# A fused test-time-memory and expert kernel: its router by VectorE's top-8 sort and first-match marking, and gates by tanh, in place of exponentials and chained reductions

## The chip, the cores and the metric

The kernel runs on one core of one Trainium2 chip. The metric is the device time of one execution in microseconds (us), and every time here is of that kind or a position in one profiled execution. A core has five engines with queues of their own: TensorE (PE; its weight loads are PEld), VectorE (DVE), ScalarE (ACT), GpSimd (POOL) and SyncE (SP), which issues the DMAs. They meet only at semaphores.

## The reference

2,048 tokens with 128 features pass through two layers, each as `x = x + layernorm(f(layernorm(x)))`. The first `f` is a memory that takes one training step on the tokens (forward, gradients, AdamW) and is then read with the new weights. The second is a mixture of 8 experts, of which each token uses 2. What concerns this case is how those two are chosen and weighted:

```python
z = _layernorm(x, ln_g, ln_b)
logits = jnp.einsum('bth,he->bte', z, rW) + rb
probs = jax.nn.softmax(logits, axis=-1)
topv, topi = jax.lax.top_k(probs, TOP_K)              # TOP_K = 2, E = 8
mask = jnp.sum(jax.nn.one_hot(topi, E) * topv[..., None], axis=-2)
w = mask / jnp.maximum(jnp.sum(mask, axis=-1, keepdims=True), 1e-08)
hid = jax.nn.gelu(jnp.einsum('bth,ehf->btef', z, W1) + b1, approximate=False)
outs = jnp.einsum('btef,efh->bteh', hid, W2) + b2
return x + jnp.sum(outs * w[..., None], axis=2)
```

The kernel computes all eight experts for every token and adds them with the weights `w`, six of which are zero.

## The kernel before, in words

The tokens form four blocks (`NB = 4`) of 512, each of four tiles (`TB = 4`) of 128 tokens. Every engine has one program, written out by hand in order, and waits on semaphores; nothing is reordered by a planner. Operations of VectorE that depend on each other are joined by a semaphore of its own (`step`, `link`, lines 709 to 719).

There are three stages. First the memory's forward and backward passes over the four blocks. Then a hinge: AdamW's new weights and, for block 0, everything that the experts need. Then 32 expert slots (`STEPS = NB * E`), which start two early (`AHEAD = 2`): in slot s TensorE makes the hidden layer of expert step s+2 (`hidden`, two halves of three 512-column products each), then the output of step s (`output`, 16 products of 128 columns), ScalarE applies Gelu to each half (`gelu`, line 682), and VectorE adds the output with its weight (`add_expert`, line 1009, four instructions at L1020). `hidden` of a block waits for `z_lo`, the low part of its normalised tokens (`z_low`, line 913, recorded at L915).

The router of a block has these steps. TensorE makes the logits in bank 4 (`logits`, line 477, recorded as L330 with `late_sb`). VectorE adds the bias and subtracts the greatest logit (`shift_logits`, line 927: L931, L935, L936). ScalarE takes exponentials of 32 values per partition (`exponentials`, line 662). VectorE then makes the weights (`route`, line 939, L960 to L994): a chain of maxima, comparisons and a rank by a descending ramp, which marks the first of equal values, with the sums and reciprocals beside it (L953). Last, TensorE transposes the weights (`w_transpose`, line 484, recorded as L487), ScalarE copies them out (`wT_out`) and TensorE multiplies them with the biases (`b2_term`).

For block 0 these steps stand in the hinge. VectorE's order there is written at lines 1051 to 1064: `... retrieve2(1); retrieve2(2); shift_logits(0); z_low(0); route(0); retrieve2(3)`. For the blocks 1 to 3 they are spread over the expert slots of the block before: `due(position, slot)` tells in which slot of that block a step is placed. Logits are at 3, `shift_logits` at 4, exponentials at 5, the first seven pieces of `route` at 5, the rest at 6, and `w_transpose` at 7. In each slot VectorE runs `add_expert` first, then what is due. In slot 6 `norm_r` of the block after the next one stands before the rest of `route` (for blocks 1 and 2; there is none for block 3).

Of the kernel before, what the change touches and what calls it, by code (L numbers as in the profile page):

```python
# [15 lines left out]
ALU = mybir.AluOpType  # L16
# [27 lines left out]
def memory_and_experts(nc, x, early, late, fW1, fW2, out):  # L44
# [19 lines left out]
    with ExitStack() as ctx:  # L64
# [58 lines left out]
        def part(pack, at, name):  # L123
# [20 lines left out]
        ramp = sb("ramp", [P, TB, E])  # L144
        lg, ex, pr, eq, oh1, oh2 = (kT[:, i * T * E:(i + 1) * T * E].rearrange("p (t e) -> p t e", e=E)
                                    for i in range(6))
        w_tok = sb("w_tok", [P, T, E])
        red = kT[:, 6 * T * E:7 * T * E].rearrange("p (i t) -> p i t", t=T)
# [6 lines left out]
        zeroed, ident_ready, half_ready, table_ready, ramp_ready = (sem(n) for n in (  # L155
            "zeroed", "ident_ready", "half_ready", "table_ready", "ramp_ready"))
# [21 lines left out]
        lg_mm, lg_shift, ex_ready, w_ready, w_tr, wT_ready = (sem(n) for n in (  # L178
            "lg_mm", "lg_shift", "ex_ready", "w_ready", "w_tr", "wT_ready"))
# [48 lines left out]
        NORM_R, RESIDUAL, NORM_Z, Y_STATS, Y_NORM, Z_LOW, LOGITS_SHIFT, ROUTE = -2, -1, 0, 1, 2, 2, 4, (5, 6)  # L228
        R_TR, Z_TR, LOGITS, EXP, W_TR, B2_TERM = -2, 2, 3, 5, 7, 8
# [55 lines left out]
        def _(pool):  # L285
# [7 lines left out]
            def rsqrt(ln, b, where=None):  # L293
# [11 lines left out]
            pool.iota(ramp[:], pattern=[[0, TB], [-1, E]], base=E, channel_multiplier=0,  # L305
                      allow_small_or_imprecise_dtypes=True).then_inc(ramp_ready, 1)
# [267 lines left out]
        def _(act):  # L574
# [87 lines left out]
            def exponentials(b):  # L662
                act.wait_ge(lg_shift, b + 1)
                act.activation(tok(ex, b), tok(lg, b), ACT.Exp).then_inc(ex_ready, 1)
# [14 lines left out]
            exponentials(0)  # L679
# [9 lines left out]
            for slot in range(-AHEAD, STEPS):  # L689
                if slot + AHEAD < STEPS:  # L690
                    for c in range(C):
                        gelu(C * (slot + AHEAD) + c)
                if slot == 0:
                    wT_out(0)
                if due(Z_TR, slot):
                    zT_out(due(Z_TR, slot))
                if due(EXP, slot):
                    exponentials(due(EXP, slot))
                if due(W_TR, slot):
                    wT_out(due(W_TR, slot))  # L700
# [3 lines left out]
        def _(dve):  # L704
# [21 lines left out]

            def advance(pieces, count):
                for _ in range(count):
                    next(pieces, None)
# [189 lines left out]
            def wide(v):  # L919
                return v.unsqueeze(2).to_broadcast([P, TB, E])  # L920

            def small(i, b):
                return red[:, i, span(b)]

            MX, SM, RS, M1, F1, M2, F2, DN = range(8)

            def shift_logits(b):
                if b == 0:
                    dve.wait_ge(ramp_ready, 1)
                dve.wait_ge(lg_mm, b + 1)  # L930
                dve.tensor_tensor(tok(lg, b), bank[4][:, 0:TB * E].rearrange("p (t e) -> p t e", e=E),  # L931
# [3 lines left out]
                yield from link(dve.tensor_reduce(small(MX, b), tok(lg, b), AX_X, ALU.max))  # L935
                dve.tensor_tensor(tok(lg, b), tok(lg, b), wide(small(MX, b)),  # L936
                                  ALU.subtract).then_inc(lg_shift, 1)

            def route(b):


                e, p, q, first, second = (tok(v, b) for v in (ex, pr, eq, oh1, oh2))
                total, inverse, top, rank, top2, denom = (small(v, b) for v in (SM, RS, M1, F1, M2, DN))
                done = {}

                def chain(ins):
                    done["chain"] = step(ins)

                def side(make, *operands, **kw):

                    if "side" in done:
                        dve.wait_ge(dve_step, done["side"])
                    done["side"] = step(make(*operands, **kw))  # L953

                def chained():
                    yield
                    dve.wait_ge(dve_step, done["chain"])

                dve.wait_ge(ex_ready, b + 1)
                chain(dve.tensor_reduce(top, e, AX_X, ALU.max))  # L960
                side(dve.tensor_reduce, total, e, AX_X, ALU.add)
                yield from chained()
                chain(dve.tensor_tensor(q, e, wide(top), ALU.is_equal))
                side(dve.reciprocal, inverse, total)
                yield from chained()
                chain(dve.tensor_tensor(q, q, ramp[:], ALU.mult))
                side(dve.tensor_tensor, p, e, wide(inverse), ALU.mult)
                yield from chained()
                chain(dve.tensor_reduce(rank, q, AX_X, ALU.max))
                yield from chained()  # L970
                chain(dve.tensor_tensor(first, q, wide(rank), ALU.is_equal))
                yield from chained()
                chain(dve.scalar_tensor_tensor(out=e, in0=first, scalar=-2.0, in1=e, op0=ALU.mult,
                                               op1=ALU.add))
                yield from chained()
                chain(dve.tensor_reduce(top2, e, AX_X, ALU.max))
                yield from chained()
                chain(dve.tensor_tensor(q, e, wide(top2), ALU.is_equal))
                side(dve.tensor_tensor, denom, top, top2, ALU.add)
                yield from chained()  # L980
                chain(dve.tensor_tensor(q, q, ramp[:], ALU.mult))
                side(dve.tensor_tensor, denom, denom, inverse, ALU.mult)
                yield from chained()
                chain(dve.tensor_reduce(rank, q, AX_X, ALU.max))
                side(dve.tensor_scalar, denom, denom, 1e-8, None, ALU.max)
                yield from chained()
                chain(dve.tensor_tensor(second, q, wide(rank), ALU.is_equal))
                side(dve.reciprocal, denom, denom)
                yield from chained()
                chain(dve.tensor_tensor(first, first, second, ALU.add))  # L990
                side(dve.tensor_tensor, p, p, wide(denom), ALU.mult)
                yield
                dve.wait_ge(dve_step, done["side"])
                dve.tensor_tensor(tok(w_tok, b), p, first, ALU.mult).then_inc(w_ready, 1)  # L994

# [65 lines left out]
            run(shift_logits(0))  # L1061
# [3 lines left out]
            for slot in range(-AHEAD, STEPS):  # L1065
# [16 lines left out]
                if due(LOGITS_SHIFT, slot):  # L1082
                    run(shift_logits(due(LOGITS_SHIFT, slot)))
                if due(ROUTE[0], slot):
                    routing = route(due(ROUTE[0], slot))
                    advance(routing, 7)
                if due(ROUTE[1], slot):
                    run(routing)
# [42 lines left out]
```

## Time and profile before

| | |
|---|---|
| median of 3 runs | 206.26 us (206.22, 206.26, 208.02) |
| the profiled execution | 204.86 us |
| its span, first to last instruction | 203.1 us |
| busy: PE / PEld | 178.0 / 140.8 us |
| busy: DVE / ACT / POOL | 145.4 / 99.1 / 22.1 us |
| mean granted TensorE clock | 0.99 |

The span leaves out what lies before the first and behind the last instruction: 1.8 us in this execution. Busy time is not the limit by itself: an engine's idle time counts only where the chain of work that ended last passes through it. "L330" is line 330 of the kernel; where a helper issues the instruction, all its uses carry the helper's line, and the names of the tiles tell them apart.

### The profile page before, as it was taken

The page shows a single profiled execution, that of the slowest core. Times are in us where ns is not written, and L with a number is a line of the kernel's source. Part 1 is how long each engine was busy: PE and PEld are TensorE (multiplying, and loading weights), DVE is VectorE, ACT ScalarE, POOL GpSimd, SP SyncE. Part 2 cuts the span into 40 slices and gives each one's busy share as a digit, 9 for nine tenths or more (in the row PEclk, how much of TensorE's full clock was granted, in tenths as well). Part 3 has the DMA queues.
Part 4 walks back from the last instruction along what each step waited for, and adds up shares of the span by engine and source line. Part 5 has one row for each costly group of instructions (what it writes and reads, how often), then busy time and mean ns, then how long its engine had stood idle before and what let it go on. Part 6 is the DMA issues. An engine that isn't in the chain of part 4 may idle for free.

```text
span 203.1 us, 3196 instructions
## 1 busy us (share of the span) xinstructions
PE 178.0 (88%) x1089; PEld 140.8 (69%) x1089; DVE 145.4 (72%) x564; ACT 99.1 (49%) x150; POOL 22.1 (11%) x30
## 2 busy tenths in 40 slices
PE   7388988897988796999999999999999999999930
PEld 7334454465644484879999699988799897889920
DVE  0987695879685799979348977668976656475474
ACT  2157682946444309934567326384355495334200
POOL 1440000000000140032000131001211000010010
PEclk9999999999999999999999999999999999999996
DMA  5970000000000000000000000100000100001001
GB/s 153 342 233 4 0 0 3 0 0 0 0 3 2 0 2 0 3 0 0 3 0 2 0 3 0 52 3 0 2 0 3 52 0 3 2 2 52 3 0 52
DMA packets 3232, 4.96 MB, mean 24 GB/s; under 512 B 240, under 2 KB 1552, under 8 KB 3216
## 3 DMA queue, kind: packets, MB, share of 16 engines
q1 hardware_dynamic: 3216, 4.76, 7.2%
q8 instruction: 9, 0.15, 0.3%
q14 instruction: 7, 0.06, 0.1%
HBM read 3.71 MB, written 1.05 MB: 23 GB/s over the span
## 4 chain that ended last, share of the span: by engine, by line
PE 69%; DVE 17%; ACT 7%; issue 3%; DMA 2%; POOL 0%; POOLq 0%; DVEq 0%; ACTq 0%
PE bank L330 65%; DVE stats L737 3%; PE bank L338 2%; DMA x_tok<-in_x_dram 2%; ACT sig L580 2%; DVE xnT L1020 2%; ACT nsig L587 2%; DVE mv L740 1%; DVE s L870 1%; DVE s L878 1%; DVE xnT L874 1%; DVE vT L881 1%; ACT s L580 1%; ACT alrT L580 1%; ACT kT L576 1%
## 5 line engine op out<-in xcount | busy, mean ns | idle before, releaser
L1020 DVE SCALAR_TENSOR_TENSOR xnT<-bank,w_tok,xnT 128x128 f32<-128x128 f32 x128 | 36.0, 344 | 27.7 <-PE bank L330 27.3
L297 POOL TENSOR_TENSOR rstd<-vpe,minus_half 128x4 f32<-128x4 f32 (+1 forms) x21 | 20.7, 995 | 175.5 <-DVE vpe L745 162.0
L330 PE MATMUL bank<-z_hi,fW_hi 128*128 128x512 f32 x64 | 27.8, 435 | 1.5 <-DVE z_lo L915 1.5
L330 PE MATMUL bank<-z_lo,fW_hi 128*128 128x512 f32 x64 | 25.2, 394 | 0.0
L330 PE MATMUL bank<-z_hi,fW_lo 128*128 128x512 f32 x64 | 25.0, 390 | 0.0
L330 PEld LDWEIGHTS bank<-fW_sb,sig 128*128 128x128 f32 x192 | 22.8, 192 | 2.2 <-ACT h1T L686 1.5
L330 PE MATMUL bank<-fW_sb,sig 128*128 128x128 f32 x192 | 23.4, 276 | 0.0
L686 ACT ACTIVATE sig<-bank,early_sb 128x512 f32<-128x512 f32 x24 | 16.2, 688 | 13.8 <-PE bank L330 13.7
L686 ACT ACTIVATE k_tok<-bank,early_sb 128x512 f32<-128x512 f32 x20 | 13.5, 688 | 15.4 <-PE bank L330 15.3
L330 PEld LDWEIGHTS bank<-fW_sb,k_tok 128*128 128x128 f32 x160 | 19.3, 191 | 1.5 <-ACT sig L686 0.8
L330 PEld LDWEIGHTS bank<-fW_sb,h1T 128*128 128x128 f32 x160 | 19.3, 191 | 1.5 <-ACT k_tok L686 0.8
L330 PE MATMUL bank<-fW_sb,h1T 128*128 128x128 f32 x160 | 19.6, 275 | 0.0
L330 PE MATMUL bank<-fW_sb,k_tok 128*128 128x128 f32 x160 | 19.6, 275 | 0.0
L686 ACT ACTIVATE h1T<-bank,early_sb 128x512 f32<-128x512 f32 x20 | 13.5, 688 | 12.3 <-PE bank L330 12.2
L330 PE MATMUL bank<-xnT,early_sb 128*128 128x512 f32 x24 | 11.9, 606 | 2.9 <-ACT alrT L580 1.3
L330 PEld LDWEIGHTS bank<-z_hi,fW_hi 128*128 128x128 f32 x64 | 12.1, 190 | 3.0 <-issue 1.6
L409 PEld LDWEIGHTS bank<-ident 128*128 128x128 f32 x93 | 11.8, 155 | 3.1 <-issue 1.6
L330 PEld LDWEIGHTS bank<-z_lo,fW_hi 128*128 128x128 f32 x64 | 12.0, 188 | 2.9
L409 PE MATMUL bank<-ident 128*128 128x128 f32 x93 | 12.5, 296 | 1.5 <-POOL ident L288 1.5
L330 PEld LDWEIGHTS bank<-z_hi,fW_lo 128*128 128x128 f32 x64 | 12.2, 190 | 1.5
L580 ACT ACTIVATE s<-bank,bn 128x512 f32<-128x512 f32 x8 | 5.5, 687 | 11.0 <-PE bank L330 11.0
L330 PEld LDWEIGHTS bank<-xnT,early_sb 128*128 128x128 f32 x24 | 4.0, 190 | 7.3 <-issue 5.7
(129 smaller groups left out, 270.4 us busy)
## 6 DMA issues: line engine op xcount, KB each, us to landing
x_tok<-in_x_dram SPq DMA_DIRECT2D x4, 256.0 KB, 4.4
fW_raw<-in_fW_dram SPq DMA_DIRECT2D x1, 1024.0 KB, 9.2
out_dram<-xn_tok SPq DMA_DIRECT2D x3, 256.0 KB, 2.5
early_sb<-in_early_dram SPq DMA_DIRECT2D x1, 268.0 KB, 4.1
late_sb<-in_late_dram SPq DMA_DIRECT2D x1, 264.0 KB, 4.8
out_dram<-xn_tok SPq DMA_DIRECT2D x2, 128.0 KB, 2.0
b_diag<-in_late_dram SPq DMA_DIRECT2D x4, 4.0 KB
fW_sb<-in_fW_dram SPq DMA_DIRECT2D x1, 0.5 KB, 11.7
```

The lines of the kernel that those rows point to most:

```text
L297: pool.tensor_tensor(rstd[:, ln, where], vpe[:, ln, where], minus_half[:, 0:where.stop - where.start], ALU.pow).then_inc(rstd_ready[ln], 1)
L330: return pe.matmul(out_, lhsT, rhs, start=start, stop=stop)
L338: last = pe.transpose(bank[7][:, i * P:(i + 1) * P], pieces(i), ident[:])
L409: pe.transpose(bank[scratch][:, 0:P], ident[:], ident[:])
L576: act.activation(dst, src, ACT.Identity, **kw).then_inc(s, 1)
L580: act.activation(cut(into, b), source[:], ACT.Sigmoid, bias=bias).then_inc(s, 1)
L587: act.activation(into[:, slot * BLOCK:(slot + 1) * BLOCK], cut(sig, b), ACT.Identity, scale=-1.0, bias=1.0).then_inc(s, 1)
L686: act.activation(g_buf[n % G_RING], bank[H_BANK[n % len(H_BANK)]][:], ACT.Gelu, bias=col(FB1 + n % UB)).then_inc(g_done, 1)
L737: last = dve.bn_stats(stats[:, t, :], source(i, t))
L740: last = dve.bn_aggr(mv[:, ln, t, :], stats[:, t, :])
L870: dve.scalar_tensor_tensor(out=cut(r_sig1, b), in0=bank[RZ1[b]][:], scalar=bn[:, 0:1], in1=cut(r_sig1, b), op0=ALU.add, op1=ALU.mult).then ...
L1020: last = dve.scalar_tensor_tensor(out=y_tok[:, t, :], in0=bank[Y_BANK[m % len(Y_BANK)]][:, i * P:(i + 1) * P], scalar=w_tok[:, t, e:e + 1] ...
```

## The change

The router's method is replaced. VectorE adds the bias, sorts the eight logits of each tile with one `max` per tile (eight values out, in falling order), copies the first two into a row whose other six places hold -3.0e38, and runs one `match_replace` per tile, which puts +3.0e38 in place of the first match of each of the eight values in the row of logits. That row is 14 wide, with six places of -3.0e38 for the fillers to match. What is now greater than the logit was chosen. The weight of a chosen expert is 0.5 * (1 + tanh(logit - half the sum of the two chosen logits)), which is its share of the two. So ScalarE takes a tanh (`Tanh`, in place, 32 values per partition) instead of exponentials, and `route` is one instruction. The tiles are arrays of their own and no longer lie in `kT`; GpSimd fills two of them once (`memset`) where it made the ramp before (`iota`).

The places: `choose(0)` stands where `shift_logits(0)` stood, ahead of `z_low(0)`; `route(0)` stays behind it. For the other blocks `choose` is at 4, the tanh at 5 and the one-instruction `route` at 5, in place of slots 5 and 6. `w_transpose` stays at 7.

```diff
-        ramp = sb("ramp", [P, TB, E])
-        lg, ex, pr, eq, oh1, oh2 = (kT[:, i * T * E:(i + 1) * T * E].rearrange("p (t e) -> p t e", e=E)
-                                    for i in range(6))
+        TOP_K, SORTED = 2, 8
+        NO_MATCH = -3.0e38
+        lg = sb("lg", [P, T, E + SORTED - TOP_K])
+        ranked = sb("ranked", [P, T, SORTED])
+        chosen = sb("chosen", [P, T, SORTED])
+        marked = sb("marked", [P, T, E + SORTED - TOP_K])
+        gate = sb("gate", [P, T, E])
+        picked = sb("picked", [P, T, E])
+        pair_sum = sb("pair_sum", [P, T])
...
-        NORM_R, RESIDUAL, NORM_Z, Y_STATS, Y_NORM, Z_LOW, LOGITS_SHIFT, ROUTE = -2, -1, 0, 1, 2, 2, 4, (5, 6)
-        R_TR, Z_TR, LOGITS, EXP, W_TR, B2_TERM = -2, 2, 3, 5, 7, 8
+        NORM_R, RESIDUAL, NORM_Z, Y_STATS, Y_NORM, Z_LOW, CHOOSE, ROUTE = -2, -1, 0, 1, 2, 2, 4, 5
+        R_TR, Z_TR, LOGITS, GATE, W_TR, B2_TERM = -2, 2, 3, 5, 7, 8
...
-            pool.iota(ramp[:], pattern=[[0, TB], [-1, E]], base=E, channel_multiplier=0,
-                      allow_small_or_imprecise_dtypes=True).then_inc(ramp_ready, 1)
+            pool.memset(lg[:], NO_MATCH).then_inc(rest_ready, 1)
+            pool.memset(chosen[:], NO_MATCH).then_inc(rest_ready, 1)
...
-            def exponentials(b):
-                act.wait_ge(lg_shift, b + 1)
-                act.activation(tok(ex, b), tok(lg, b), ACT.Exp).then_inc(ex_ready, 1)
+            def gate_tanh(b):
+                act.wait_ge(gate_in, b + 1)
+                act.activation(tok(gate, b), tok(gate, b), ACT.Tanh).then_inc(gate_ready, 1)
...
-            def shift_logits(b):
+            def choose(b):
+
                 if b == 0:
-                    dve.wait_ge(ramp_ready, 1)
+                    dve.wait_ge(rest_ready, 2)
                 dve.wait_ge(lg_mm, b + 1)
-                dve.tensor_tensor(tok(lg, b), bank[4][:, 0:TB * E].rearrange("p (t e) -> p t e", e=E),
+                dve.tensor_tensor(lg[:, span(b), 0:E], bank[4][:, 0:TB * E].rearrange("p (t e) -> p t e", e=E),
                                   rb_b.unsqueeze(1).to_broadcast([P, TB, E]), ALU.add).then_inc(lg_read, 1)
                 yield
                 dve.wait_ge(lg_read, b + 1)
-                yield from link(dve.tensor_reduce(small(MX, b), tok(lg, b), AX_X, ALU.max))
-                dve.tensor_tensor(tok(lg, b), tok(lg, b), wide(small(MX, b)),
-                                  ALU.subtract).then_inc(lg_shift, 1)
+                for t in tiles(b):
+                    last = dve.max(ranked[:, t, :], lg[:, t, 0:E])
+                yield from link(last)
+                copied = step(dve.tensor_scalar(chosen[:, span(b), 0:TOP_K], ranked[:, span(b), 0:TOP_K], 1.0, None,
+                                                ALU.mult))
+                yield from link(dve.tensor_tensor(pair_sum[:, span(b)], ranked[:, span(b), 0],
+                                                  ranked[:, span(b), 1], ALU.add))
+                dve.scalar_tensor_tensor(out=tok(gate, b),
+                                         in0=pair_sum[:, span(b)].unsqueeze(2).to_broadcast([P, TB, E]),
+                                         scalar=-0.5, in1=lg[:, span(b), 0:E], op0=ALU.mult,
+                                         op1=ALU.add).then_inc(gate_in, 1)
+                dve.wait_ge(dve_step, copied)
+                for t in tiles(b):
+                    last = dve.match_replace(marked[:, t, :], chosen[:, t, :], lg[:, t, :], -NO_MATCH)
+                yield from link(last)
+                yield from link(dve.tensor_tensor(tok(picked, b), marked[:, span(b), 0:E], lg[:, span(b), 0:E],
+                                                  ALU.is_gt))
+                yield from link(dve.tensor_scalar(tok(picked, b), tok(picked, b), 0.5, None, ALU.mult))
 
             def route(b):
-                e, p, q, first, second = (tok(v, b) for v in (ex, pr, eq, oh1, oh2))
...
-                dve.tensor_tensor(tok(w_tok, b), p, first, ALU.mult).then_inc(w_ready, 1)
+                dve.wait_ge(gate_ready, b + 1)
+                dve.scalar_tensor_tensor(out=tok(w_tok, b), in0=tok(gate, b), scalar=1.0, in1=tok(picked, b),
+                                         op0=ALU.add, op1=ALU.mult).then_inc(w_ready, 1)
+                yield
...
-            run(shift_logits(0))
+            run(choose(0))
             z_low(0)
             run(route(0))
...
-                if due(LOGITS_SHIFT, slot):
-                    run(shift_logits(due(LOGITS_SHIFT, slot)))
-                if due(ROUTE[0], slot):
-                    routing = route(due(ROUTE[0], slot))
-                    advance(routing, 7)
-                if due(ROUTE[1], slot):
-                    run(routing)
+                if due(CHOOSE, slot):
+                    run(choose(due(CHOOSE, slot)))
+                if due(ROUTE, slot):
+                    run(route(due(ROUTE, slot)))
```

## Rows read from the trace of the kernel before

**Rows 1.** The page: span, and part 1, busy time, share, instructions by engine

```profile
span 203.1 us, 3196 instructions
PE 178.0 (88%) x1089; PEld 140.8 (69%) x1089; DVE 145.4 (72%) x564; ACT 99.1 (49%) x150; POOL 22.1 (11%) x30
```

**Rows 2.** The chain that ended last: start us, us, what; hinge, and slots 6 and 7

```profile
79.57 0.20 DVE kT L931
79.79 0.20 DVE kT L935
...
80.21 0.61 DVE z_lo L915
...
80.96 1.63 PE bank L330 x6
...
113.02 0.20 DVE w_tok L994
...
113.27 0.28 PE bank L487
```

**Rows 3.** Who waited for whom: us in total, times, longest us

```profile
PE bank L330 <- DVE z_lo L915: 1.5, 1, 1.5
...
PE bank L487 <- DVE w_tok L994: 0.7, 2, 0.4
```

**Rows 4.** Timeline, all engines, hinge: start, us, engine, line, operation [idle before, releaser]

```profile
78.51 0.95 PE L330 MATMUL bank<-late_sb,alrT 128*128 128x8 f32 x8
...
79.56 1.28 ACT L664 ACT_TABLE_LOAD   x1
79.57 0.19 DVE L931 TENSOR_TENSOR kT<-bank,late_sb 128x32 f32<-128x32 f32 x1
...
80.12 0.69 DVE L915 TENSOR_TENSOR z_lo<-alrT,z_hi 128x512 fp32r<-128x512 f32 x1
...
80.96 0.47 PE L330 MATMUL bank<-z_hi,fW_hi 128*128 128x512 f32 x1 [1.50 <-DVE z_lo L915]
81.11 1.28 ACT L686 ACT_TABLE_LOAD   x1
```

**Rows 5.** VectorE's groups, shapes apart: line, operation, shapes, count, busy us, mean ns

```profile
L740 DVE BATCH_NORM_AGGREGATE mv<-stats 128x2 f32<-128x6 f32 x64 | 6.1, 157 | 0.5
...
L971 DVE TENSOR_TENSOR kT<-kT 128x32 f32<-128x32 f32 x4 | 0.8, 192 | 0.1
```

**Rows 6.** Timeline of VectorE: four L740 in a row, then the next, dependent one

```profile
73.71 0.38 DVE L740 BATCH_NORM_AGGREGATE mv<-stats 128x2 f32<-128x6 f32 x4
74.12 0.17 DVE L905 TENSOR_SCALAR vpe<-mv 128x4 f32<-128x4 f32 x1
```

**Rows 7.** Timeline of TensorE: last output before w_transpose, blocks 1 and 3

```profile
110.98 1.95 PE L330 MATMUL bank<-fW_sb,sig 128*128 128x128 f32 x16
113.27 0.28 PE L487 MATMUL bank<-ident,w_tok 128*32 128x128 f32 x1 [0.35 <-DVE w_tok L994]
...
168.61 1.95 PE L330 MATMUL bank<-fW_sb,k_tok 128*128 128x128 f32 x16
170.39 0.27 PE L487 MATMUL bank<-ident,w_tok 128*32 128x128 f32 x1
```

**Rows 8.** Timeline, block 1's slots 4 and 5: ScalarE's load, VectorE's additions

```profile
104.05 0.18 DVE L931 TENSOR_TENSOR kT<-bank,late_sb 128x32 f32<-128x32 f32 x1
...
105.10 1.28 ACT L664 ACT_TABLE_LOAD   x1
...
106.18 1.13 DVE L1020 SCALAR_TENSOR_TENSOR xnT<-bank,w_tok,xnT 128x128 f32<-128x128 f32 x4 [1.50 <-PE bank L330]
```

**Rows 9.** Stretches at the end: stretch, length, busy of each engine, PEclk, DMA share, GB/s

```profile
196.00:198.00 2.00, 0.00 (x0) 0.00 (x0) 1.25 (x11) 0.00 (x0) 0.97 (x2) 1.00 0.00 0
198.00:200.00 2.00, 0.00 (x0) 0.00 (x0) 1.57 (x8) 0.00 (x0) 0.39 (x1) 0.79 0.00 0
200.00:203.00 3.00, 0.00 (x0) 0.00 (x0) 0.48 (x2) 0.00 (x0) 0.00 (x0) 0.50 0.26 87
```

More of the change, by code:

```diff
@@ L143, in memory_and_experts @@
         minus_half = sb("minus_half", [P, TB])
-        ramp = sb("ramp", [P, TB, E])
-        lg, ex, pr, eq, oh1, oh2 = (kT[:, i * T * E:(i + 1) * T * E].rearrange("p (t e) -> p t e", e=E)
-                                    for i in range(6))
+        TOP_K, SORTED = 2, 8
[7 more added lines that the diff above has]
+        pair_sum = sb("pair_sum", [P, T])
         w_tok = sb("w_tok", [P, T, E])
-        red = kT[:, 6 * T * E:7 * T * E].rearrange("p (i t) -> p i t", t=T)
         x_in = [sem(f"x_in{i}") for i in range(NB)]
@@ L153, in memory_and_experts @@
         out_done = sem("out_done")
-        zeroed, ident_ready, half_ready, table_ready, ramp_ready = (sem(n) for n in (
-            "zeroed", "ident_ready", "half_ready", "table_ready", "ramp_ready"))
+        zeroed, ident_ready, half_ready, table_ready, rest_ready = (sem(n) for n in (
+            "zeroed", "ident_ready", "half_ready", "table_ready", "rest_ready"))
         b2_zeroed, b2_in, fw_hi_done, fw_lo_done = (sem(n) for n in (
@@ L177, in memory_and_experts @@
                              "zT_ready", "zhi_done", "zlo_done"))
-        lg_mm, lg_shift, ex_ready, w_ready, w_tr, wT_ready = (sem(n) for n in (
-            "lg_mm", "lg_shift", "ex_ready", "w_ready", "w_tr", "wT_ready"))
+        lg_mm, gate_in, gate_ready, w_ready, w_tr, wT_ready = (sem(n) for n in (
+            "lg_mm", "gate_in", "gate_ready", "w_ready", "w_tr", "wT_ready"))
         rs1_done, rs2_done, shift_ready, lg_read, dp_done = (sem(n) for n in (
@@ L678, in _ @@
             rsig2_out(3)
-            exponentials(0)
+            gate_tanh(0)
             def gelu(n):
@@ L696, in _ @@
                     zT_out(due(Z_TR, slot))
-                if due(EXP, slot):
-                    exponentials(due(EXP, slot))
+                if due(GATE, slot):
+                    gate_tanh(due(GATE, slot))
                 if due(W_TR, slot):
@@ L725, in run @@
                     pieces = [p for p in pieces if next(p, "end") != "end"]
-            def advance(pieces, count):
-                for _ in range(count):
-                    next(pieces, None)
             def span(b):
@@ L916, in z_low @@
                                   ALU.subtract).then_inc(zlo_done, 1)
[L919 to L925, printed above, removed]
-            def shift_logits(b):
+            def choose(b):
                 if b == 0:
-                    dve.wait_ge(ramp_ready, 1)
+                    dve.wait_ge(rest_ready, 2)
                 dve.wait_ge(lg_mm, b + 1)
-                dve.tensor_tensor(tok(lg, b), bank[4][:, 0:TB * E].rearrange("p (t e) -> p t e", e=E),
+                dve.tensor_tensor(lg[:, span(b), 0:E], bank[4][:, 0:TB * E].rearrange("p (t e) -> p t e", e=E),
                                   rb_b.unsqueeze(1).to_broadcast([P, TB, E]), ALU.add).then_inc(lg_read, 1)
@@ L934, in shift_logits @@
                 dve.wait_ge(lg_read, b + 1)
-                yield from link(dve.tensor_reduce(small(MX, b), tok(lg, b), AX_X, ALU.max))
-                dve.tensor_tensor(tok(lg, b), tok(lg, b), wide(small(MX, b)),
-                                  ALU.subtract).then_inc(lg_shift, 1)
-            def route(b):
-                e, p, q, first, second = (tok(v, b) for v in (ex, pr, eq, oh1, oh2))
[L943 to L991, printed above, removed]
@@ L992, in route @@
                 yield
-                dve.wait_ge(dve_step, done["side"])
-                dve.tensor_tensor(tok(w_tok, b), p, first, ALU.mult).then_inc(w_ready, 1)
             def start_sum(j):
```

## The prediction

> **What bounds the kernel now.** I read the page first. TensorE is busy 88% of the span, VectorE 72%, ScalarE 49% [rows 1]. No share says what an edit of the router is worth; that takes the places where the chain of waits passes through the router. There are two kinds. In the hinge the chain runs through VectorE: the bias addition at 79.57, the maximum at 79.79, then `z_low` of block 0, and from 80.96 through TensorE's first hidden product [rows 2]. In the expert slots it is on TensorE, except for the end of `route`: it passes w_tok (L994) at 113.02 and reaches w_transpose at 113.27 [rows 2].
>
> The list of waits gives the size. Once TensorE waits for z_lo, 1.5 us, and twice for w_tok, 0.7 us together [rows 3]. In the expert part, from 81 to 194, TensorE has no other wait in that list. So ScalarE's and VectorE's work in there is hidden, and only these three waits can answer to the edit.
>
> The timeline of the hinge shows that the first wait is one of VectorE alone. TensorE ends its logits at 78.51 + 0.95 = 79.46 and sits still until 80.96; the table load and exponentials on ScalarE lie beside that [rows 4].
>
> **The change part by part. First, `choose(0)` ahead of `z_low(0)`.** Before, z_low starts at 80.12, which is 0.55 us after the bias addition [rows 4]: two dependent steps and the start of the third instruction. Afterwards all of `choose` comes first, as `run` goes through to its end, and the last step waits as well.
>
> The prices come from small operations. A dependent step of 32 values starts 0.22 us after the one before it (79.57 to 79.79) [rows 2]; the durations behind this are 192 ns for 32 values and 157 ns for the smallest forms [rows 5]. Without dependence they overlap: four of 157 ns take 0.38, so each starts (0.38 - 0.16) / 3 = 0.075 after the last, and the dependent one follows 0.03 after the end [rows 6]. No row shows a `max` or a `match_replace`. I take them as records of some 8 to 16 values, about 165 ns, starting 0.08 apart, nearest to the 157 ns rows. A match_replace I count as two records, since it has to take in eight values to look for before it passes the row. That gives:
>
> bias addition 0.22; four max 3 x 0.08 + 0.20 = 0.44; the copy 0.08 and the dependent pair sum 0.19, 0.27; the tanh's input 0.11; eight records of match_replace 7 x 0.08 + 0.20 = 0.76; the comparison and the halving 0.45. The sum is 2.25 us.
>
> So z_low starts 2.25 - 0.55 = 1.70 us later, and so does the first hidden product, since nothing else is due later: TensorE stands idle already. From below, a match_replace is one record like L740, and so is a max: 0.22 + 0.41 + 0.27 + 0.11 + 0.41 + 0.45 = 1.87, a delay of 1.3. From above, none of the twelve overlap and each takes a whole dependent step of 0.22: 0.22 + 0.88 + 0.27 + 0.11 + 1.76 + 0.45 = 3.69, a delay of 3.1. I take 1.70, nearer to the lower end, because all small operations in the rows overlap.
>
> On the two records there is a sentence in the Trainium skill, page VectorE: DVE Perf Modes, section "Two Vector instructions with no wait between them": it lists `MATCH_VALUE_LOAD` and `MATCH_REPLACE_8` as two instructions with one input each. No row here shows either. By one record for each match_replace at 0.08 the sum would be 1.93 and the delay 1.4; by the page it stays as above.
>
> **Second, w_transpose at slot 7.** Before, the second half of `route` ran in slot 6 behind norm_r and ended at 113.2 in block 1. From the start of the last output products to w_transpose takes 113.27 - 110.98 = 2.29 us there, and 170.39 - 168.61 = 1.78 in block 3, where no norm_r stands before it and TensorE does not wait [rows 7]. Block 2 repeats block 1 (2.30). So the two waits cost 0.51 and 0.52: their ends on the list are shorter (0.35 each), because the overlap with the product before is lost too. Afterwards w_tok of block 1 is ready in slot 5: `choose` starts at about 104.05 [rows 8] and ends near 106.3; the tanh's input is there about 1.1 us after the start, at 105.2, when ScalarE is just through with its two Gelus (it began its load at 105.10 [rows 8]); tanh ends at 105.5; and `route`, one instruction behind the additions at 106.18 to 107.31, ends by 107.7, five us ahead of w_transpose. Both stalls go: -1.03 us. Behind them the list has nothing that is late next.
>
> What `choose` pushes back in slot 4: the additions of slot 5 started at 106.18 after 1.50 us of idle waiting for TensorE [rows 8], so 2.25 us of work from 104.05 makes them some 0.15 late. The output that needs their bank begins at 110.98 [rows 7], over three us after they end, so this costs nothing; even 3.7 us of work would leave two.
>
> **Third, ScalarE.** Four loads of 1.28 us before the exponentials and four behind them, back to Gelu's table, may go wholly or down to one. In the hinge the load back ends at 81.11 + 1.28 = 82.39 [rows 4] while hidden products run from 80.96; TensorE's list shows no wait for a Gelu there. In the slots it idles anyway, and TensorE waits for none [rows 3]. I take 0. Should tanh still need loads, the load and tanh end at about 106.6 in block 1, before `route` comes up at 107.3; in the hinge the first hidden product ends after 83 and the loads before it. Also 0, so this term doesn't depend on the tables.
>
> The rest: VectorE has some 24 router records per block before and 19 after, and in the hinge route(0) shrinks from 3 us to 0.2. That follows z_low, where TensorE did not wait for it, so it only widens the margin in front of the first w_transpose. GpSimd's two fills stand where the ramp stood, far ahead of 79.5. Both 0.
>
> **Sum.** +1.70 - 1.03 = +0.67 us. The profiled execution takes 204.86, its span 203.1 and 1.8 around it; it becomes 205.5. The median of the runs is 1.4 higher at 206.26, and the forecast is made against it: 206.9 us.
>
> **The rivals.** (A) The clock falls in the hinge: the case on the other side, slower by over 1%. TensorE's idle time there grows from 1.5 to 3.2 us. At the end of the kernel the last product ends at about 194.5; the granted clock is still 1.00 until 198, 0.79 on average from 198 to 200, and 0.50 behind that [rows 9], so it fell to its lower level (1.2 of 2.4 GHz) some 4.6 us after the last work. 3.2 us is less, but these rows hold one fall only, and TensorE's work before this gap is thinner than at the end. The upper end of my delay, 3.1, would make the gap 4.6 us, just there. From that point the first slots run at half speed. The price: from 80.96 to the end of the first output at 87.40 TensorE has 6.4 us of dense work; half to all of 3.2 us of it twice over adds 1.6 to 3.2, say 2.4. With the delay that is 206.26 + 0.67 + 2.4 = 209.3; with the slow instructions as well 210.7. Chance 0.10. The page TensorE: Matmul & The Clock Gate of the Trainium skill, section "HAM oscillation — how this bites in real kernels", warns of this kind of idle gap in TensorE's work; the rows here show the gate closing only at the end.
>
> (B) Sorting and marking are dear, without a fall of the clock: a delay of 2.3 to 3.1, net +1.3 to +2.1, some 207.9. For it: a sort of eight is not like any operation in the rows. Chance 0.15.
>
> (C) They are cheap, or the hinge hides part: a delay of 1.0 to 1.3. Net 0 to +0.3, time 206.4. It speaks for it that the least shapes give 1.87 us. Chance 0.15.
>
> (D) VectorE's total counts, not the place: 5 records per block fewer, and 1.0 us from w_transpose, and the hinge pays under 0.5 because z_low is overtaken by something I have not seen. Then it is faster, by 0.5 to 1.5 us: 205.2. Against it: z_low is the only releaser of the first hidden product in the list [rows 3]. The page VectorE: DVE Perf Modes, section "Rules for kernel authors", says to minimise the count of chained operations; by count alone this change should gain. Chance 0.08, and half of that or more within 1%.
>
> (E) The stalls at w_transpose remain, because tanh is late or w_tok is held: +1.7, 208.0. The margin of five us speaks against it. Chance 0.05.
>
> The forecast itself holds 0.47, with its own range of 206.5 to 207.4.
>
> **How the numbers follow.** About 1%, 2.1 us, is what a measurement of this kernel can tell from no change. Faster by more than that needs (D) beyond its own bound or runs that scatter: 0.04. Slower by more, from 208.3: (A), the end of (B), some of (E), 0.14. Within: 0.82. The range takes (C) and most of (B) and (D), and leaves out most of (A): 205.6 to 208.6.
>
> **What would show it.** In the changed profile: z_low of block 0 starting 2.0 to 2.5 us after the bias addition and the wait for z_lo grown from 1.5 to about 3.2; no wait for w_tok in the list and 1.78 us from the last output's start to each w_transpose; no table load between Gelus, or loads without any effect; granted clock 1.00 from 80 to 90. I am wrong if a max or a match_replace lasts over 0.2 us, if the delay in the hinge is below 1.0, or if the clock falls there.

## The result and the profile after

| | before | after |
|---|---|---|
| median of 16 runs each | 205.75 us | 206.85 us |
| lowest | 204.49 us | 205.16 us |
| ratio, with its 95% interval | | 1.0077 [1.0049, 1.0106] |
| profiled execution / its span | 204.86 / 203.1 us | 207.73 / 205.9 us |
| mean granted clock of that execution | 0.99 | 0.97 |

The change makes the kernel 0.8% slower by the ratio, 1.6 us, and 1.1 us by the two medians; the forecast was 0.3% slower. Runs of one kernel lie in groups, and this case can't be read without them: of the kernel before, seven of 16 took 204.5 to 204.8 us, the others 205.7 and more; of the changed kernel one took 205.16, nine 206.6 to 206.9, and the rest more. The reason, as far as the profiles show it, is TensorE's clock, below.

The page of the changed kernel, span and part 1, answers to [rows 1]:

```profile
span 205.9 us, 3171 instructions
PE 181.2 (88%) x1089; PEld 143.4 (70%) x1089; DVE 141.1 (69%) x544; ACT 90.6 (44%) x143; POOL 22.3 (11%) x31
```

VectorE has 20 instructions and 4.3 us less to do, ScalarE 8.5 us less, and the span is longer. TensorE has the same 1,089 products and is busy 3.2 us longer with them: its products became slower, and the forecast's sum had no term for that (its rival (A) had).

The chain that ended last, in the hinge (start us, us, what), answers to [rows 2]:

```profile
80.34 0.20 DVE lg L925
80.54 0.02 issue
80.56 0.39 DVE ranked L930 x4
80.95 0.02 issue
80.97 0.17 DVE chosen L932
81.14 0.08 DVE pair_sum L934
81.22 0.02 issue
81.24 0.19 DVE gate L936
81.44 0.58 DVE marked L942 x5
82.02 0.02 issue
82.04 0.20 DVE picked L944
82.24 0.02 issue
82.27 0.19 DVE picked L946
82.46 0.02 issue
82.48 0.70 DVE z_lo L916
83.18 0.14 issue
83.32 1.91 PE bank L335 x6
85.22 0.85 PE bank L467 x4
86.08 3.67 PE bank L335 x12
89.74 0.11 PE bank L492
```

The whole of `choose` now stands in the chain in front of z_low, step by step. From the bias addition to z_low it is 82.48 - 80.34 = 2.14 us, where it was 0.55 [rows 4]: a delay of 1.59. The list of TensorE's waits from 79 us to 200 us, which answers to [rows 3], has one line left:

```profile
PE bank L335 <- DVE z_lo L916: 3.1, 1, 3.1
```

It grew from 1.5 to 3.1, and both waits for w_tok are gone. The timeline of TensorE at the end of slot 7 in block 1 answers to [rows 7]: 116.72 - 114.93 = 1.79 us, as block 3 had before, instead of 2.29. Blocks 2 and 3 of the changed kernel have 1.78.

```profile
114.93 1.95 PE L335 MATMUL bank<-fW_sb,sig 128*128 128x128 f32 x16
116.72 0.27 PE L492 MATMUL bank<-ident,w_tok 128*32 128x128 f32 x1
```

The clock is what the sum lacked. The stretches of the changed kernel around the hinge (stretch, length, busy us of PE, PEld, DVE, ACT, POOL with counts, PEclk, DMA share, GB/s):

```profile
80.00:82.00 2.00, 0.23 (x3) 0.14 (x2) 1.88 (x17) 0.82 (x3) 0.00 (x0) 1.00 0.00 0
82.00:84.00 2.00, 0.68 (x3) 0.63 (x4) 1.86 (x7) 1.00 (x1) 0.00 (x0) 1.00 0.00 0
84.00:86.00 2.00, 2.00 (x10) 1.62 (x9) 0.66 (x1) 1.37 (x2) 0.00 (x0) 0.62 0.03 8
86.00:88.00 2.00, 2.00 (x7) 1.56 (x6) 1.44 (x9) 0.60 (x1) 0.29 (x1) 0.53 0.00 0
88.00:90.00 2.00, 2.00 (x12) 1.60 (x11) 1.25 (x6) 1.68 (x4) 0.71 (x1) 1.00 0.00 0
```

From 84.5 to 87.9 the clock is at its lower level, 1.2 of 2.4 GHz (a mean of 0.62 is 1.5 us at half, one of 0.53 is 1.9 us). It falls 4.3 us after TensorE's last work at 80.23, and when it falls TensorE has been at work again for 1.2 us. The first w_transpose in the timeline of TensorE, of the kernel before:

```profile
85.62 0.27 PE L487 MATMUL bank<-ident,w_tok 128*32 128x128 f32 x1
```

and of the changed kernel:

```profile
89.58 0.27 PE L492 MATMUL bank<-ident,w_tok 128*32 128x128 f32 x1
```

From the first hidden product to it the changed kernel takes 89.58 - 83.32 = 6.26 us, the kernel before 85.62 - 80.96 = 4.66 [rows 4]: 1.60 more.

The two profiled executions then compare so: 1.59 in the hinge, 1.60 by the clock, -1.03 at w_transpose, and 0.77 from before the router (the bias addition itself comes at 80.34 instead of 79.57), together 2.9, against 2.8 between the spans. The last term is not the change's. Most of it is an earlier fall of the same clock, from 9.4 to 12.8 us, which this execution had and that of the kernel before had not. It comes and goes with either router: below, the old router's profiles with the delay and with `route` in slot 5 have it, and two profiles with the new router (22 fillers, Exp for Tanh) have not.

### The profile page after: what moved, and what is told of

Its sections match the earlier page's. It is cut to its first block, busy times and chain, and to the rows that moved or that the text cites. A ratio compares the mean times of both kernels' runs of the same rounds, so it can differ in the third digit from the quotient of the medians.

```text
span 205.9 us, 3171 instructions
## 1 busy us (share of the span) xinstructions
PE 181.2 (88%) x1089; PEld 143.4 (70%) x1089; DVE 141.1 (69%) x544; ACT 90.6 (44%) x143; POOL 22.3 (11%) x31
## 3 DMA queue, kind: packets, MB, share of 16 engines
HBM read 3.71 MB, written 1.05 MB: 23 GB/s over the span
## 4 chain that ended last, share of the span: by engine, by line
PE 73%; DVE 14%; ACT 6%; issue 2%; DMA 2%; POOL 0%; POOLq 0%; DVEq 0%; ACTq 0%
PE bank L335 68%; PE bank L343 3%; DVE stats L738 2%; DMA x_tok<-in_x_dram 2%; ACT sig L585 2%; ACT nsig L592 2%; PE bank L467 1%; DVE s L871 1%; DVE s L879 1%; DVE xnT L875 1%; DVE vT L882 1%; DVE mv L741 1%; ACT s L585 1%; ACT alrT L585 1%; PE bank L479 1%
## 5 line engine op out<-in xcount | busy, mean ns | idle before, releaser
L335 PE MATMUL bank<-z_hi,fW_hi 128*128 128x512 f32 x64 | 28.4, 443 | 3.1 <-DVE z_lo L916 3.1
L335 PE MATMUL bank<-z_lo,fW_hi 128*128 128x512 f32 x64 | 25.7, 402 | 0.0
L335 PE MATMUL bank<-z_hi,fW_lo 128*128 128x512 f32 x64 | 25.5, 398 | 0.0
L335 PE MATMUL bank<-xnT,early_sb 128*128 128x512 f32 x24 | 12.9, 648 | 2.9 <-ACT alrT L585 1.3
L414 PEld LDWEIGHTS bank<-ident 128*128 128x128 f32 x93 | 12.5, 161 | 3.1 <-issue 1.6
L414 PE MATMUL bank<-ident 128*128 128x128 f32 x93 | 13.2, 306 | 1.5 <-POOL ident L293 1.5
```

Source lines behind the costliest of these rows:

```text
L335: return pe.matmul(out_, lhsT, rhs, start=start, stop=stop)
L414: pe.transpose(bank[scratch][:, 0:P], ident[:], ident[:])
```

## The experiments

Each experiment has 6 to 12 runs. Where a kernel has runs without a fall of the clock, its lowest run should be one of them, so differences of lowest runs come nearest to the work alone, and ratios show both. The kernel with the delay and that with Exp for Tanh have no run that looks like one without a fall.

| run | lowest us | median us | ratio to before [95%] |
|---|---|---|---|
| the changed kernel | 205.16 | 206.85 | 1.0077 [1.0049, 1.0106] |
| z_low first | 203.63 | 204.85 | 0.9952 [0.9911, 0.9992] |
| changed, gap filled with 44 | 206.60 | 206.96 | 1.0079 [1.0047, 1.0112] |
| old router, delay in front of z_low | 207.77 | 209.35 | 1.0179 [1.0128, 1.0230] |
| old router, route in slot 5 | 203.47 | 204.92 | 0.9952 [0.9911, 0.9992] |
| changed, gap filled with 22 | 205.10 | 206.23 | 1.0016 [0.9977, 1.0054] |
| z_low first, tanh behind Gelu | 202.72 | 203.38 | 0.9883 [0.9829, 0.9937] |
| the same, z_low earliest | 202.42 | 203.57 | 0.9862 [0.9815, 0.9910] |
| old router in these places | 203.48 | 204.58 | 0.9933 [0.9898, 0.9969] |
| changed, Exp for Tanh | 206.59 | 207.53 | 1.0088 [1.0049, 1.0128] |
| old router, z_low first | 204.47 | 205.17 | 0.9994 [0.9945, 1.0043] |

The kernel before ran again beside the first four experiments, the next four and the last two. Its lowest runs there were 204.52, 204.55 and 204.55, its medians 206.13, 206.10 and 206.08.

**z_low first.**

```diff
-            run(choose(0))
             z_low(0)
+            run(choose(0))
```

> The changed kernel with z_low(0) moved ahead of choose(0), nothing else. My theory: the changed kernel pays in the hinge because z_low of block 0 starts 2.14 us after the bias addition instead of 0.55, and pays again because the longer idle time of TensorE (3.1 us) is followed by about 3.3 us at half clock. With z_low first, it starts at once, TensorE's wait shrinks to about 0.9 us, no half clock between 80 and 90; the weights are still ready ahead of w_transpose. Expected 0.55 + 1.03 us faster than the kernel before, about 1.6 us, and some 3.2 below the changed kernel. Rival (sorting and marking or the tanh are dear wherever they stand): still not below the kernel before.

The delay is gone and with it the fall of the clock in the hinge: granted 1.00 from 80 to 90 in its profile. The kernel is faster than both others, but by 0.9 us at the lowest run, not 1.6. The list of TensorE's waits from 78 to 90 us shows why:

```profile
PE bank L335 <- DVE z_lo L916: 0.8, 1, 0.8
PE bank L335 <- ACT sig L691: 0.4, 1, 0.4
```

A wait for the first Gelu is new. ScalarE's timeline gives its cause:

```profile
82.17 0.23 ACT L669 ACTIVATE gate<-gate 128x32 f32<-128x32 f32 x1 [1.64 <-DVE gate L936]
82.42 1.28 ACT L691 ACT_TABLE_LOAD   x1
83.71 2.43 ACT L691 ACTIVATE sig<-bank,early_sb 128x512 f32<-128x512 f32 x4
```

ScalarE sits on the tanh's input, and Gelu's table is loaded only behind it, so the first Gelu starts at 83.71 though its product began at 81.27. From the first hidden product to w_transpose it is 5.34 us instead of 4.66: 0.68 given back, more than the 0.4 in the list; the overlap with the product before is lost as well. So the hinge gives nothing net against the kernel before, and the gain is that at w_transpose.

**The delay alone, with the old router.**

```diff
             run(shift_logits(0))
+            for _ in range(7):
+                run(link(dve.tensor_tensor(spare[:], late_sb[:, 0:32], late_sb[:, 0:32], ALU.add)))
             z_low(0)
```

> The kernel before, its old router untouched, with seven dependent additions of 32 values on VectorE, results unused, between shift_logits(0) and z_low(0): about 1.55 us, which is the delay that the changed kernel has there. My theory: the place alone costs, so the clock falls behind it as in the changed kernel and this one is 1.6 + 1.6 = 3.2 us slower than the kernel before. Rival (the loss is of the sort and mark instructions themselves, and delay at this place costs only its own length): 1.6 us slower, or less if something absorbs it.

Its timeline has the seven additions, 1.53 us, and TensorE's wait is 3.1 us, that of the changed kernel:

```profile
81.47 1.53 DVE L1064 TENSOR_TENSOR spare<-late_sb 128x32 f32<-128x32 f32 x7
```

It is 3.2 us slower at the lowest run (207.77 against 204.52), twice the delay's length. The clock of its profiled execution, one of 210.31 us, is at the lower level from 82.6 to 89.4, so here it fell during the wait (to 83.87):

```profile
82.00:84.00 2.00, 0.13 (x1) 0.16 (x1) 1.83 (x10) 1.70 (x3) 0.00 (x0) 0.64 0.00 0
...
88.00:90.00 2.00, 2.00 (x8) 1.58 (x7) 1.36 (x10) 0.77 (x2) 0.49 (x1) 0.65 0.00 0
```

```profile
83.87 0.77 PE L331 MATMUL bank<-z_hi,fW_hi 128*128 128x512 f32 x1 [3.07 <-DVE z_lo L916]
...
91.11 0.27 PE L488 MATMUL bank<-ident,w_tok 128*32 128x128 f32 x1
```

From the first hidden product to w_transpose it is 91.11 - 83.87 = 7.24 us, 2.58 more than before: this fall lasted 6.8 us, twice as long as that of the changed kernel, and cost 2.6 us and not 1.6. The lowest run has no profile; the 1.7 us that it loses beyond the delay are like a fall of the shorter kind. So the sort and the marking need no cost of their own kind to explain the loss: 1.53 us of plain VectorE work at this place cost 3.2 at the lowest run.

**The gap filled.** First with 44 transposes, which was too many; then the same line with 22.

```diff
             logits(0)
+            keep_clock(3, 44)
```

> The changed kernel with 44 transposes of the identity put on TensorE behind logits(0), which fill some 2.4 us of the 3.1 us in which it waits for z_low; no order of the real work changes. My theory: half of the loss in the hinge is the clock. Then the clock stays at 1.00 from 80 to 90, the first eight products keep their full speed, and the time is about 1.6 us below the changed kernel, some 0.6 above the kernel before. Rival (the clock falls for what TensorE did before the gap, or whatever it does, or the loss is VectorE's alone): the fall stays and the time is that of the changed kernel.

> The changed kernel with 22 transposes of the identity behind logits(0); in the run with 44 each took 0.11 us, so 44 held the first product up to 85.23 though z_low had long been done. 22 last 2.4 us and end before z_low does. My theory: half of the hinge's loss is the clock, which falls in nearly every run of the changed kernel. Then the clock is 1.00 from 80 to 90 in the profile and the time falls by up to 1.6 us to +0.6 over the undisturbed level of the kernel before, near 205.2 in most runs. Rival (fillers don't count, or the clock falls by what lies before): no change against the changed kernel, 206.8.

With 44 the clock held, at 1.00 from 78 to 90, but the fillers themselves kept TensorE until 85.23 (row below), as each takes 0.11 us, and the gain went into that: the expected 1.6 us did not come, since the experiment was wrongly sized.

```profile
80.47 5.00 PE L414 MATMUL bank<-ident 128*128 128x128 f32 x44
85.23 0.47 PE L335 MATMUL bank<-z_hi,fW_hi 128*128 128x512 f32 x1
```

With 22 the wait for z_lo that is left is 0.64 us and the clock is at 1.00 from 80 to 90:

```profile
79.67 2.60 PE L414 MATMUL bank<-ident 128*128 128x128 f32 x22
82.91 0.47 PE L335 MATMUL bank<-z_hi,fW_hi 128*128 128x512 f32 x1 [0.64 <-DVE z_lo L917]
```

Five of twelve runs took 205.1 to 205.7 us, against one of 16 of the changed kernel, and the level is the same as that one, 0.6 above the lowest of the kernel before: 1.59 - 1.03, the sum of the forecast. Four more took 206.2 to 206.4, which is this level and the 1.2 us of the early fall, which the fillers don't touch; the changed kernel has no run between 205.2 and 206.6. The last three, 206.9 to 207.8, and one of 206.71 look like the fall in the hinge again, alone or with the other. These readings are from times, as only the run of 205.70 has a profile; its last logits start at 78.86 us, 0.4 to 0.6 later than in the other profiles without a fall in front, which is most of its distance from 205.1. The ratio went from 1.0077 to 1.0016.

**Only the place of `route`, old router.**

```diff
-        ... LOGITS_SHIFT, ROUTE = -2, -1, 0, 1, 2, 2, 4, (5, 6)
+        ... LOGITS_SHIFT, ROUTE = -2, -1, 0, 1, 2, 2, 4, (5, 5)
```

> The kernel before with the second half of route moved from slot 6 to slot 5, the old router untouched. My theory: the two stalls at w_transpose are a matter of its place behind norm_r, worth 0.51 us each, so this alone makes the kernel before 1.0 us faster and the list shows no wait for w_tok. Rival (the longer VectorE work in slot 5, 2.9 us, pushes the additions of slot 6 and takes it back): within 0.3 us of the kernel before.

No wait for w_tok is left in the list, and the lowest run is 1.05 us below that of the kernel before, the ratio 0.9952. So the 1.03 us that the change gained in the slots are gained without any new instruction. This profile also caught the clock's fall (at 81.8 us) at the end of a wait of only 1.5 us, the same wait as that of the kernel before, whose profile has no fall there:

```profile
80.00:82.00 2.00, 0.50 (x5) 0.44 (x4) 1.67 (x5) 1.97 (x3) 0.00 (x0) 0.94 0.00 0
82.00:84.00 2.00, 2.00 (x5) 1.61 (x6) 1.79 (x14) 1.76 (x3) 0.00 (x0) 0.50 0.04 8
84.00:86.00 2.00, 2.00 (x9) 1.59 (x9) 1.93 (x11) 0.94 (x2) 0.00 (x0) 0.71 0.00 0
```

**The tanh behind the first Gelus**, on top of z_low first; and **z_low earliest**, inside `retrieve2(2)`.

```diff
             rsig2_out(3)
-            gate_tanh(0)
...
                         gelu(C * (slot + AHEAD) + c)
+                if slot == -AHEAD:
+                    gate_tanh(0)
```

> z_low(0) ahead of choose(0), and on ScalarE the tanh of block 0 behind the first two Gelus instead of ahead of them. With z_low first alone TensorE had a new wait of 0.41 us for the first Gelu, since ScalarE held the tanh until 82.17 and only then loaded Gelu's table. My theory: the load now runs as soon as the last sigmoid is done, the wait of 0.41 goes, one load is left in the whole expert part, and the time is 0.4 us below z_low first alone. Rival (tanh behind the Gelus makes the weights late for w_transpose, or asks for a load of its own): no gain, with a wait for w_tok in the list.

```diff
             def retrieve2(b):
...
+                if b == 2:
+                    z_low(0)
                 dve.wait_ge(rs2_done, b + 1)
```

> As the run with the tanh behind the Gelus, but z_low(0) stands inside retrieve2(2), between its two instructions, as soon as the high part is there. My theory: TensorE's wait in the hinge falls to about 0.3 us, 0.5 less than with z_low first; the weights still come in time. Against the kernel before: 1.2 us in the hinge and 1.0 at w_transpose, 2.2 us faster. Rival (VectorE is the bound in the hinge by its total, 14% of the chain, so work that is only moved comes back): w_transpose or the first output waits, and the time is that of z_low first.

The second went as expected; the first gained more. It is 0.9 us below z_low first at the lowest run, where 0.4 was expected: from the first hidden product to w_transpose it takes 86.02 - 81.35 = 4.67 us, so the whole 0.68 is back and not only the wait of 0.41. The other 0.2 is not explained. In its profile the load stands ahead of the tanh and the first Gelu follows its product:

```profile
80.62 1.28 ACT L690 ACT_TABLE_LOAD   x1
82.32 1.37 ACT L690 ACTIVATE sig<-bank,early_sb 128x512 f32<-128x512 f32 x2 [0.42 <-PE bank L335]
83.59 0.22 ACT L669 ACTIVATE gate<-gate 128x32 f32<-128x32 f32 x1
```

This is the only load in the expert part: tanh needs none behind a Gelu, nor does a Gelu behind such a tanh. (With z_low first alone the tanh ran before Gelu's table was loaded, and the Gelu then needed the load.) In the second the wait for z_lo is 0.38 us, and the lowest run is 202.42, 2.1 us below that of the kernel before, as worked out. With a ratio of 0.9862 [0.9815, 0.9910] it beats both kernels. Against the first of these two the gain of 0.3 us shows at the lowest runs only; the medians, of six runs each, don't.

**The old router in the same places.** As the kernel before, with `route` wholly in slot 5 and z_low(0) inside `retrieve2(2)`; its exponentials stay where they were.

> The old router with the same places: route wholly in slot 5 and z_low(0) inside retrieve2(2). It tells what the new router is worth once place costs neither anything. My theory: in the hinge the exponentials' two table loads keep the first Gelu until about 82.4, so TensorE, which now starts near 79.8, waits about 0.9 us for it, and the old router is about 0.9 us slower than the new one in the same places; against the kernel before it is 1.0 + 0.3 us faster. Rival (the loads hide here as they did before): as fast as the new router in these places.

```profile
PE bank L330 <- ACT sig L686: 0.6, 1, 0.6
PE bank L330 <- DVE z_lo L917: 0.4, 1, 0.4
```

It waits for the first Gelu as expected; from the first hidden product to w_transpose it takes 85.11 - 79.61 = 5.50 us, against 85.45 - 80.80 = 4.65 with the new router. The lowest runs are 1.06 us apart and the medians 1.01, of which these 0.85 explain the greater part. So about 1 us is what the new router is worth in these places, and the profile shows it where the gate's table is loaded, not in VectorE's time. Against the old router with only `route` moved, 203.47, the earlier z_low gained nothing (203.48). One rival wasn't run: the old router with its exponentials behind the first Gelus, as the tanh stands here.

**Exp for Tanh, and z_low first with the old router.**

```diff
-                act.activation(tok(gate, b), tok(gate, b), ACT.Tanh).then_inc(gate_ready, 1)
+                act.activation(tok(gate, b), tok(gate, b), ACT.Exp).then_inc(gate_ready, 1)
```

> The changed kernel with Exp in place of Tanh, nothing else (so the gates are other numbers). It brings the table loads back: one pair in each of the four blocks. My theory: with z_low behind choose the loads are hidden everywhere, since in the hinge the first hidden product comes only at about 83 and in the slots no one waits for the Gelus; the time is that of the changed kernel within 0.3 us, and nothing of the change's 1.1 to 1.6 us is tanh's. Rival (the eight loads' 10 us on ScalarE are worth something in the slots): slower than the changed kernel by 0.5 us or more, with waits of TensorE for a Gelu.

This kernel's gates are other numbers, so only its time counts. The loads come back, and no wait of TensorE with them:

```profile
L669 ACT ACT_TABLE_LOAD x4 | 5.1, 1283 | 0.1
L691 ACT ACT_TABLE_LOAD x4 | 5.1, 1283 | 0.1
```

The lowest run, 206.59, lies with the first of the changed kernel's group from 206.6 to 206.9, and the ratios are 1.0088 and 1.0077. Its profile has the fall in the hinge (83.4 to 86.8) and none in front, at 206.73 us: 1.6 above the one low run of the changed kernel. As the change was written, tanh is worth nothing that these runs can tell, some 0.3 us at most.

> The kernel before with z_low(0) ahead of shift_logits(0), nothing else. My theory: the first hidden product starts 0.6 us earlier, but the exponentials and with them Gelu's table come 0.6 us later, so TensorE waits some 0.6 us for the first Gelu at its fourth product: no gain, within 0.2 us of the kernel before. So z_low first pays only with a gate that needs no load of its own. Rival (z_low first pays for itself): 0.6 us faster, no wait for a Gelu.

Against the kernel before, the lowest run is 0.08 us lower and the ratio 0.9994: no gain at the lowest run, as expected, though the interval allows half a per cent either way. The reason is another than expected. The load of the exponentials' table ended at 80.56 and held them, so they came no later for z_low's going first; Gelu's table was ready at 82.10 (82.39 before, where the logits too came 0.29 later), and the hidden products reached it earlier. From the first hidden product to w_transpose it takes 85.06 - 80.01 = 5.05 us; 0.39 of the 0.67 gained in front is given back there. The profile would leave 0.28, the lowest runs show 0.08. The waits for w_tok stay in the list.

## Why the prediction was right, and where it was not

**The place of the cost: right.** z_low is the only releaser of the first hidden product, and `choose` is in the chain with its whole length. The delay was forecast at 1.70 and is 1.59 us, of 2.14 instead of 2.25. With 1.59 and no wait for w_tok, rivals (B), (C) and (E) fell. The difference of the lowest runs, 205.16 - 204.49 = 0.67, is the forecast's sum, though the changed kernel has only one such run.

**The prices of the unknown records: right, by part.** VectorE's groups of the changed kernel, shapes apart, answer to [rows 5]:

```profile
L942 DVE MATCH_REPLACE8 marked<-chosen,lg 128x14 f32<-128x14 f32 x16 | 2.3, 159 | 0.0
L930 DVE MAX8 ranked<-lg 128x8 f32<-128x8 f32 x16 | 1.5, 156 | 0.1
L942 DVE MATCH_VALUE_LOAD marked<-chosen,lg 128x8 f32 x16 | 1.3, 83 | 0.0
```

Two records for each match_replace, as the Trainium skill's VectorE: DVE Perf Modes, section "Two Vector instructions with no wait between them", has it; the trace agrees. Taken at 0.08 each, they start 0.07 apart, since the load of values takes 83 ns and not 165. From the first load to the comparison it is 0.69 us (0.76 in the sum); the four max with their wait are 0.41 (0.44).

**w_transpose: right.** -1.03 us in the sum, 2.29 to 1.79 in the rows, and 1.05 in the run that changes nothing else.

**ScalarE: right for this change, wrong as a rule.** Its loads were costed at 0, and Exp for Tanh shows that. The cover was z_low's lateness. With z_low earlier the same term is 0.4 to 0.9 us (0.39, 0.68 and 0.85 in three profiles), and the tanh's place decides whether it is paid.

**The clock: the step that failed.** The main forecast has the granted clock at 1.00 from 80 to 90, and names its fall there as a sign of being wrong: it fell. Rival (A) was given 0.10 and, as the times are read, happened in 15 of 16 runs. The forecast held the one fall in [rows 9], 4.6 us after TensorE's last work, against a wait of 3.2 us and took the first for a limit that the second keeps. The rows now show that it isn't one: the clock fell here 1.2 us after the wait had ended, in the old router with a delay during a wait of 3.1 us, and in the old router with `route` in slot 5 at the end of a wait of 1.5. With the longer wait nearly all runs have the time of a fall, with that of the kernel before a part of them. What decides it in one execution stays open. The price was estimated at 2.4 us and is 1.60 here, 1.5 and 1.6 in two of the experiments' profiles, and 2.6 in that with the delay. The warning of the Trainium skill's TensorE: Matmul & The Clock Gate, section "HAM oscillation — how this bites in real kernels", against idle gaps in front of TensorE's work holds in this kernel, by the stretch from 84.5 to 87.9. The gaps in or behind which the clock fell, 3.1 us here and 1.5 with `route` in slot 5, are shorter than the one that the page warns of, and the measurement decides. That the runs' median, 206.85, is the forecast's 206.9 is luck: the median of the kernel before was 206.26 in the runs shown and 205.75 in all 16. Of the difference, the forecast had 0.67 where the ratio gives 1.6. An estimate of the rest: 1.59 - 1.03 = 0.56 is the work, and about 1.0 is the fall's 1.6 us in some six of ten runs more than before.

**Rival (D), VectorE's total counts: fell.** 20 instructions fewer show no gain outside the two places, and the old router with only its place changed gained all of the 1.03.

## What to carry to other kernels

Cheaper work can cost time by its place: of an edit, first ask which of its instructions stand in front of what another engine waits for, and whether they must. Here the operand of the waiting product depended on nothing in the router, and one line moved turned 0.8% of loss into 0.5% of gain. Where TensorE's wait in front of dense work grows, price a fall of its clock beside the delay: here it was 1.6 to 2.6 us on top of 1.5 to 1.6. Filling the gap avoided it in the profile, but fill no more of it than there is. A table load that is hidden behind one wait has to be priced again as soon as that wait is gone.

## What the runs showed of the hardware that was not expected

The granted clock can fall after TensorE has resumed its work: at 84.5 us, with products running since 83.32. It then stayed at the lower level for 3.4 us of dense work. In the kernel with the delay it fell about 1.8 us after the last work, at 82.6, and rose at 89.4. It is not a matter of the program alone: the kernel before and the one with `route` in slot 5 are alike up to the hinge, and their wait of 1.5 us had no fall in one profile and one in the other; the fall between 9 and 15 us comes and goes likewise. That fits the groups of run times in the kernel before: 204.6 without a fall, 205.6 to 206.4 with one, 207.3 to 207.5 with both. The profiled executions bear it out. Those with the early fall alone lie 1.2 to 1.4 us above the lowest run of their kernel (203.63 to 204.86, 202.42 to 203.60, 202.72 to 204.16), that with both, old router and `route` in slot 5, 2.8 above (203.47 to 206.25). For runs without a profile it is read from the time; the mean granted clock doesn't tell the groups apart (205.7 us stands beside 0.984 and beside 0.976). Times above 207.7 of the kernel before are not explained.

A transpose of the identity in float32 took 0.11 us when TensorE did nothing else (44 in 5.00 us, 22 in 2.60), and 4.8 us of nothing but these kept the granted clock at 1.00.
